# Routing steps of the third and fourth token group in later slots of a hand-laid program, and the direct first projections one slot later

## The reference

```python
Q, K, V = (proj(Wq, bq), proj(Wk, bk), proj(Wv, bv))
attn = softmax(einsum('bhqd,bhkd->bhqk', Q, K) * scale)
x = _layernorm(x + (attended @ Wo + bo))
...
shared_out = silu(xf @ sw1) * (xf @ sw3) @ sw2
s = sigmoid(xf @ router_w.T)
_, topk_idx = top_k(s + router_bias, 2)            # 2 of 8 experts
gates = s_sel / (s_sel.sum(axis=1) + 1e-9)         # or 1/2 each
comb = einsum('nke,nk->ne', one_hot(topk_idx), gates)
h = gelu(einsum('nd,edh->neh', xf, ew1))
routed_out = einsum('ned,ne->nd', einsum('neh,ehd->ned', h, ew2), comb)
x = _layernorm(x + shared_out + routed_out)
```

## Time and profile before

| | |
|---|---|
| median of 3 runs | 224.44 us (223.92 to 226.66) |
| the profiled execution | 224.54 us, its span 222.7 us |
| PE | 204.2 us busy, 92% of the span |
| DVE | 155.4 us, 70% |
| ACT | 138.2 us, 62% |
| POOL | 127.1 us, 57% |
| mean granted TensorE clock | 0.983 |

### The profile page before, as it was taken

How to read it: one execution, slowest core, us unless ns; L and a number is a source line. 1 busy time by engine, 2 the same in 40 slices (tenths; PEclk the granted TensorE clock), 3 DMA queues, 4 the chain that set the end, 5 groups by cost and what they waited for, 6 DMA issues and landing times.

```text
span 222.7 us, 4566 instructions
## 1 busy us (share of the span) xinstructions
PE 204.2 (92%) x1564; PEld 120.3 (54%) x1564; DVE 155.4 (70%) x319; ACT 138.2 (62%) x280; POOL 127.1 (57%) x248
## 2 busy tenths in 40 slices
PE   7999989899999999999999999999899588999980
PEld 7765564345455555555545555556365256556760
DVE  6678888779998999999963443773834545654664
ACT  2699697887879787887875767343684223344330
POOL 8687899348779868965296544805607540200203
PEclk9999999999999999999999999999999979999996
DMA  4291374376420000000280008100026006510011
GB/s 142 85 272 38 103 216 113 101 217 231 106 57 3 0 10 3 6 0 9 50 333 12 0 4 315 65 0 0 0 121 262 0 0 259 169 31 16 3 47 47
DMA packets 10358, 19.19 MB, mean 86 GB/s; under 512 B 1920, under 2 KB 6912, under 8 KB 9696
## 3 DMA queue, kind: packets, MB, share of 16 engines
q1 hardware_dynamic: 8912, 17.06, 23.4%
q10 hardware_dynamic: 1040, 1.05, 1.4%
q0 software_dynamic: 384, 0.79, 1.3%
HBM read 12.80 MB, written 1.11 MB: 62 GB/s over the span
## 4 chain that ended last, share of the span: by engine, by line
PE 61%; DVE 17%; POOL 10%; issue 5%; ACT 4%; DMA 1%; POOLq 0%; DVEq 0%
PE pv_bank L892 11%; PE ring L866 8%; PE max_bank L1049 6%; DVE top L744 6%; PE sum_bank L1049 4%; PE sum_bank L866 3%; POOL qstack L427 3%; PE max_bank L875 2%; PE pv_bank L900 2%; PE misc_bank L982 2%; PE ring L844 2%; PE ring L846 2%; PE ring L845 2%; PE misc_bank L971 2%; PE ring L943 1%
## 5 line engine op out<-in xcount | busy, mean ns | idle before, releaser
L744 DVE TENSOR_REDUCE top<-max_bank 128x2 f32<-128x512 f32 x128 | 80.5, 683 | 11.2 <-PE max_bank L875 11.2
L638 ACT ACTIVATE probs_mem<-ring 128x512 f32<-128x512 f32 x86 | 49.0, 599 | 15.6 <-PE ring L866 7.4
L875 PE MATMUL max_bank<-kstack,qstack 32*128 32x256 f32 x256 | 41.3, 328 | 0.7 <-DVE top L744 0.4
L892 PE MATMUL pv_bank<-probs_mem,v 128*18 128x256 f32 x512 | 40.1, 385 | 0.5 <-ACT probs_mem L638 0.2
L866 PE MATMUL ring<-qstack,kstack 32*128 32x256 f32 x172 | 35.0, 326 | 1.7 <-DVE top L744 1.7
L814 DVE TENSOR_TENSOR probs_mem<-xt,gates_mem 128x512 f32<-128x512 f32 (+1 forms) x34 | 22.7, 671 | 19.4 <-ACT xt L718 18.5
L1049 PE MATMUL max_bank<-probs_mem,wf 128*128 128x512 f32 (+1 forms) x60 | 28.1, 551 | 4.1 <-DVE probs_mem L814 3.2
L638 ACT ACTIVATE probs_mem<-sum_bank 128x512 f32<-128x512 f32 x42 | 25.1, 598 | 7.2 <-PE ring L866 6.9
L718 ACT ACTIVATE xt<-ring 128x512 f32<-128x512 f32 (+1 forms) x26 | 14.6, 563 | 24.0 <-PE ring L846 23.6
L875 PEld LDWEIGHTS max_bank<-kstack,qstack 32*128 32x128 f32 x256 | 25.7, 183 | 6.0 <-POOL kstack L538 1.8
L866 PEld LDWEIGHTS ring<-qstack,kstack 32*128 32x128 f32 x172 | 21.2, 183 | 13.3 <-issue 6.5
(11 more groups left out here) (190 smaller groups left out, 398.5 us busy)
## 6 DMA issues: line engine op xcount, KB each, us to landing
gates_mem<-gate_scratch SPq DMA_DIRECT2D x4, 2048.0 KB, 7.8
kstack<-gates_mem SPq DMA_DIRECT2D x36, 64.0 KB, 2.6
qstack<-gates_mem SPq DMA_DIRECT2D x24, 64.0 KB, 2.1
wf<-w_ffn_dram SPq DMA_DIRECT2D x1, 1408.0 KB, 6.9
xs<-x_dram SPq DMA_DIRECT2D x4, 256.0 KB, 5.7
xt<-x_t_dram SPq DMA_DIRECT2D x3, 256.0 KB, 4.4
qstack<-gates_mem POOLq DMA_DIRECT2D x12, 64.0 KB, 2.3
out_dram<-xs SPq DMA_DIRECT2D x3, 256.0 KB, 2.3
```

What stands on the lines that cost most here:

```text
L638: nc.scalar.activation(probs[:, i % 2, s_heads(s)[r], :], ring_of["scores", 2 * s + r][:, :], ACT.Exp, scale=SCALE).then_inc(probs_made, 1)
L744: dve.tensor_reduce(top[:, b % 2, m_heads(m)[r], t, :], max_bank[(2 * m + r) % NMAX][:, :].rearrange("p (h k) -> p h k", h=2), AX.X, ALU.m ...
L875: ins = mm(max_bank[(2 * m + r) % NMAX][:, qt * S:(qt + 1) * S], qstack[rows, t, q:q + P], kstack[rows, t, b * S:(b + 1) * S], start=True, ...
L892: ins = mm(pv_bank[32 * j:32 * j + 2 * VW, 0:S], v[:, (QT * b + kt) * H // 2 + HPS * n + j, k * VW:(k + 2) * VW], probs[:, p // 2 % 2, j, ...
```

## The change

No instruction is added or removed, and no tile changes its size. Some jobs move to other slots.

- Group 2 (`b` = 5 in the loop): route0, sig, route1, route2, route3, rank, route4, den, route5 stood in tail + 0, 0, 1, 1, 2, 3, 4, 4, 5. They now stand in tail + 0, 1, 1, 2, 3, 4, 5, 6, 6. combT 2 goes from tail + 6 to + 7; load gates 2 stays in + 8.
- Group 3: they stood in tail + 8, 8, 9, 9, 10, 11, 12, 12, 13, and now stand in + 8, 9, 9, 10, 11, 12, 13, 15, 15. combT 3 goes from + 14 to + 18, load gates 3 from + 15 to + 19.
- Start: first 4, 5, 6 and 7 go one slot later, so that first 4 no longer shares first 3's slot.
- The misc banks are dealt out in order of use, so three uses get another bank: router 7 pv_bank and combT 2 max_bank, the "third" of unit 23 misc_bank where it was pv_bank (the bank of unit 22's), and finT 1 pv_bank.

```diff
-                   (2, ("first", 3)), (2, ("first", 4)), (3, ("first", 5)), (4, ("first", 6)), (5, ("first", 7)), (7, ("k", 1)),
+                   (2, ("first", 3)), (3, ("first", 4)), (4, ("first", 5)), (5, ("first", 6)), (6, ("first", 7)), (7, ("k", 1)),
...
+    late = dict(route0=0, sig=1, route1=1, route2=2, route3=3, rank=4, route4=5, den=6, route5=6)
...
-                put(first + 15 + (n if b < 5 else (n + 1) // 2), (kind, b // 2))
+                put(first + 15 + n if b < 5 else NHALF + late[kind], (kind, b // 2))
...
-                   (6, ("combT", 2)), (8, ("load gates", 2)), (14, ("combT", 3)), (15, ("load gates", 3))):
+                   (7, ("combT", 2)), (8, ("load gates", 2)), (18, ("combT", 3)), (19, ("load gates", 3))):
...
-        put(NHALF + 7 + (n + 1) // 2, (kind, NG - 1))
+        put(NHALF + 8 + late[kind] + (n > 9), (kind, NG - 1))
```

## The result

The changed kernel takes 217.36 us in the median of six runs (216.58 to 219.59), beside 224.60 us for the kernel before (223.92 to 226.66): a ratio of 0.968, 95% interval 0.962 to 0.974. The forecast was 218.0 in a range of 216.6 to 220.8, and faster. The profiled execution took 217.16 us, its span 215.3.

What follows compares the result with a forecast made beforehand. PE, busy 92% of the span, was taken as the bound, so only its holes could be won. From 224.5 us, 1.0 (first knot), 4.9 (second knot, net) and 0.6 (start) came off, giving 218.0; range 216.6 to 220.8.

Steps and rivals of the forecast that it cites:

- First knot: Group 2's routing near 155 us: PE's waits of 0.92 and 0.28 us for DVE products vanish; net gain 1.0 us.
- The charge of 0.2 us for combT 2: At unit 16: ACT's copy of combT 2 comes between router 7's exponential and the gelu's table load, costing 0.2 us.
- the walk: In the tail: PE and DVE followed through the new order with the earlier trace's durations; 0.5 us allowed each way.
- Second knot: Group 3's routing near 175 us: PE's wait for unit 20's product falls from 2.4 to 0.4 us; gain 5.0 us by down 23.
- POOL's run: Group 3's route1 to route3 on POOL: starts about 170.0 us, still takes 6.21 us, ends at 176.2.
- So 1.8 us are the clock and 3.1 the waits: Group 3's net gain of 4.9 us split: 1.8 us from low clock behind PE's 2.37 us hole, 3.1 from waits.
- the clock, 1.8: Behind a large PE hole in the tail: TensorE's granted clock drops, adding 1.8 us to a rival's price.
- the rival in which the wait only moves: In group 3, POOL's run lengthens or rank 3 delays unit 21's product too much: 220.0 to 221.8 us; chance 0.19.
- Group 3's gates: Load for unit 32's product: slack 0.5 us; as a rival it comes late, 218.7 to 219.5 us, chance 0.10.
- The start: First projections: m = 5 ends earlier, 0.6 us gained; rival that it brings nothing, 218.6 us, chance 0.09.
- nothing with a fixed time holds them, so 0.6 us stays: After the first scores: the stage is paced by PE and DVE, so the start's 0.6 us lasts to the end.
- the missing loss of 0.1 behind down 23: Before down 26: combT 3's PE work no longer falls in a hole, so 0.1 us is lost.

Runs made afterwards that it cites:

- e8: The changed kernel with combT 2 and its gates load two slots later (tail + 9 and + 10); ratio 0.968 to the kernel before.
- e4: The kernel before, nothing moved, with seven extra unused products filling PE's wait ahead of unit 20's down product; ratio 0.9995.
- e2: The kernel before with only group 2's routing steps and combT 2 moved; ratio 0.994.
- e6: The changed kernel with rank 3 one slot earlier, ahead of finT 0 and unit 20's product; ratio 0.989 to the kernel before.
- e7: The changed kernel with route4 3 and den 3 directly behind rank 3 and route5 3 one slot on; ratio 0.977 to the kernel before.
- e5: The changed kernel with combT 3 and group 3's gates load two slots later (tail + 20 and + 21); ratio 0.987 to the kernel before.
- e1: The kernel before with only first projections 4 to 7 one slot later; ratio 0.998.
- e11: The changed kernel run once more, unaltered, as base on the same chip; ratio 0.973 to the kernel before, median 218.33 us.
- e9: The changed kernel with the first projections back in their old slots; ratio 0.974 to the kernel before, median 218.75 us.
- e3: The kernel before with only group 3's routing steps, combT 3 and its load moved; ratio 0.977.

## Why the prediction was right, and where it was not

- **First knot, 1.0 us forecast, 1.13 measured** (1.09 with group 2 alone). Both holes closed, rank 2 found its input ready, and so did den 2 at 156.90. The gain is made of 1.20 - 0.42 = 0.78 us of holes and 0.35 us of PE's own busy time (26.24 for 26.59 us by the windows), which I had not counted and which the rows explain only in part (a down product behind a hole shows 1.13 or 1.10 us, one without 1.02). The charge of 0.2 us for combT 2 between the router's exponential and the gelu was right: PE waits 0.17 us at down 16. The 0.25 us at combT 2 itself are a wait that the walk did not have: it is for POOL's `comb`, whose steps now stand behind POOL's part of yT 7. e8 shows both gone when combT 2 moves away.
- **Second knot, 5.0 us forecast, 4.99 measured.** On the clock of the kernel before (2.41 us later than after's, by PE's readiness for down 20, 175.10 to 172.69) the walk stands against the trace like this: start of POOL's run 170.0 forecast, 169.7 measured; rank 3 at 176.2, 176.0; down 20 at 175.5, 175.46; unit 21's product done at 177.3, 177.04; down 23 at 182.35, 182.35. The wait at rank 3 was forecast at 0.7 and is 0.62. The hole at down 20 was forecast at 0.4 and is 0.36; that at down 23 was 0.24, not 0.7, since PE's own work in between was a little longer than its sum of durations.
- **The split of that gain was wrong.** The step "So 1.8 us are the clock and 3.1 the waits" took the time that the slow products needed (4.1 us for work of 2.26) for time lost. e4 restores the clock and gains no time that can be measured, and e2's profile without the low clock comes to combT 3 at the same distance from rank 3. PE's slowness was covered by the chain rank 3 to `comb`, which had 7.9 us of its own. The 5.0 us came from taking this chain off PE's path, by the order of rank 3 behind finT 0 and by putting combT 3 behind down 23. The sum was not hurt, because it was a walk of the new order and not a sum of removed waits. The rivals priced "the clock, 1.8" from this step; in the changed order, where no other chain covers it, e6 has such a price, 1.64 us, so their figure was near, though not for its reason.
- **Price of a moved wait.** e6 and e7 give two prices for the rival in which the wait only moves: 4.9 us for a job one slot too early, with a hole of 3.56 us and the clock's 1.64, and 1.8 us for den 3 too near. The forecast for that rival was 2.0 to 3.8 us.
- **POOL's run.** The row of `sel` starts at 167.28 and that of `diff` at 172.53 ends at 173.58 (timeline of POOL after), 6.30 us for the 6.21 of the earlier trace rows:

```profile
167.28 0.25 POOL L581 TENSOR_TENSOR sel<-sig,brow 128x32 f32<-128x32 f32 x1 [5.07 <-DVE sig L786]
...
172.53 1.05 POOL L598 TENSOR_TENSOR diff<-diff,tie 128x256 f32<-128x256 f32 x1
```

  The rule of the Trainium skill, "GPSIMD Engine Reference", section 8 (Key points), on contention with VectorE was the mechanism behind the rival. The run was only 0.09 us longer, but three of DVE's products with two inputs from SBUF stand beside it in both kernels (from 168.94 to 172.23 before, from 168.25 to 172.34 after), so the run does not test the rule. Single steps of POOL do, and the trace agrees. Timelines of DVE (unit 24's and 25's products) and of POOL (three steps of route5 3) after:

```profile
181.31 0.69 DVE L815 TENSOR_TENSOR probs_mem<-xt,gates_mem 128x512 f32<-128x512 f32 x1
182.44 0.69 DVE L815 TENSOR_TENSOR probs_mem<-xt,gates_mem 128x512 f32<-128x512 f32 x1 [0.44 <-ACT xt L719]
```

```profile
181.36 0.74 POOL L609 TENSOR_TENSOR picked<-picked,den_inv 128x32 f32<-128x32 f32 x1
182.17 0.24 POOL L611 TENSOR_TENSOR mask<-mask,equal_share 128x32 f32<-128x32 f32 x1
182.49 0.75 POOL L615 TENSOR_TENSOR comb<-picked,mask 128x32 f32<-128x32 f32 x1
```

  A step that starts beside such a product ends 0.1 us after it and shows 0.74 or 0.75 us; alone the same steps take 0.24 and 0.25 (`comb` of group 2, at 161.46). So in all thirteen profiles: in the tail `comb` takes 0.74 or 0.75 us beside an L815 and 0.25 without, and 0.25 too beside the products of shared units (L807, L810), which read one input from PSUM. The walk had no such term. It made `comb` of group 3 ready at 183.24, 3.3 us after unit 23's result and not 2.8, and left combT 3 (at 183.71) 0.5 us of cover instead of 0.8. `den_inv` of group 2 took 0.75 us instead of 0.20 in the same way (160.00), more than the 0.25 us by which combT 2 then waited; no run takes that one apart.
- **Group 3's gates.** Forecast slack 0.5 us. The load is issued at 186.50 (timeline of SP after) and landed 7.8 us later, at 194.3; unit 32's product starts at 194.67.

```profile
186.50 0.33 SPq L478 DMA_DIRECT2D gates_mem<-gate_scratch  x1
```

```profile
gates_mem<-gate_scratch SPq DMA_DIRECT2D x1, 2048.0 KB, 7.8
```

  So the slack was 0.4 us. Over all thirteen profiles this one load landed after 7.0 to 7.8 us; the 9.0 of the earlier trace rows belongs to another group's. With the load 3.8 us later (e5) it cost 4.9 us in the profiled execution.
- **The start, 0.6 us forecast.** The mechanism and the size at the first scores were right (0.64). The step that failed is "nothing with a fixed time holds them, so 0.6 us stays": PE then runs ahead of the landings of POOL's transfers (0.58 us in e1, 0.43 in e11), and at unit 3's triple the six undisturbed profiles with the changed start lie at 130.29 to 130.67 and e11 at 130.84, beside 130.72 in the only undisturbed one without it. So 0.17 us are left in the mean of the seven, and what remains is not settled. With times alone (e1 0.998, e9 beside e11 0.4 us) even nothing is not excluded. Between the two profiled executions the gap between forecast and time is filled by the way to m = 0, 0.95 us in favour of the changed kernel by chance. Without it the profiles differ by 6.45 us, beside a forecast of 6.5, in which the first knot's 0.1 too little and the missing loss of 0.1 behind down 23 make up for most of what the start did not bring: that the sum came out so close is in part luck.

## What to carry to other kernels

When two engines hand a small result back and forth, the cost is not their work but what is queued behind the one that waits: put each step of the receiver where the sender is done by the trace's durations, and let work that nobody waits for stand ahead of it. Price a new order by walking the engine that bounds through it, not by adding up the waits that disappear: a slow stretch that ends in a wait for another chain costs next to nothing, and will cost in full once that chain is gone. After such a move look at once for the latest transfer with the least cover, and measure its slack; here it is 0.4 us, and a load 3.8 us later cost 3.6 to 4.9 us. Where POOL runs small steps of such a chain, count 0.5 us more for each that begins beside a product of DVE with both inputs in SBUF.

## What the runs showed that I had not expected

- **One hole, two clocks.** Behind a hole of 2.37 us the granted clock of the next 4.0 us was 0.57 (before), behind one of 2.43 us it was 1.00 (e2). Holes of 2.39 us gave 0.71 and 0.80 over the following 5.9 us (e2, e4), 2.72 gave 0.72 (e5), 3.56 gave 0.60 (e6), 1.49 gave 1.00 (e7). The Trainium skill, "TensorE: Matmul & The Clock Gate", Part 1, has activity release the clock; these rows agree in direction, and in e2 the first hole was followed by no low clock.
- **A low clock without a hole.** In e9 the clock was 0.54 over 7.5 us in which PE was busy throughout. e2, e3, e4 and e7 have a stretch of it in the attention stage, with 0.9 to 3.7 us more there. It is as deep and only shorter: in e2 the clock was 0.50 from 80 to 82 us, in e3 from 68 to 70, with PE busy 2.00 of the 2 us both times and no wait of PE over 0.22 us in the 4 us ahead. In e7 it was 0.50 from 80 to 86 us, and there a wait of 0.87 us for a transfer ended at 80.14. It would fit the spread of single times (the changed kernel took 216.93 us at a mean clock of 0.995 and 219.59 at 0.987), but what sets it off stays open.
- **The way to m = 0** varies by 1.5 us between executions of programs that are the same up to there.
